# A two-layer cross-attention kernel: the last chunk's layer 0 placed directly behind chunk 6's, ahead of chunk 4's layer 1, with chunk 6's layer 1 behind the last norm and a fourth x2 buffer

## What is computed

```python
# layer 0
qkv = ln(x, g1, be1) @ w_qkv + b_qkv
ckv = context @ w_ckv + b_ckv
k, v = concat(k_self, k_ctx), concat(v_self, v_ctx)
attn = softmax(where(causal or context, q k^T / sqrt(8), -inf)) @ v
x = x + attn
hdn = gelu(ln(ln(x, g2, be2), gf, bf) @ w1 + b1)
x = x + hdn @ w2 + b2
# layer 1
q = ln(x, ln_w, ln_b) @ wq.T + bq;  k, v = context @ wk.T + bk, context @ wv.T + bv
out = softmax(where(mask == 0, -1e9, q k^T / sqrt(8))) @ v @ wo.T + bo + x
```

## Time and profile before

| what | value |
|---|---|
| median of 3 executions | 466.83 us (463.14 to 469.13) |
| the profiled execution, its own time | 466.68 us |
| its span, first to last instruction | 464.7 us |
| around the span | 2.0 us |
| busy share: TensorE matmul / VectorE / ScalarE / GpSimd | 83% / 63% / 56% / 31% |
| mean granted TensorE clock, of full speed | 0.920 |
| instructions | 20173 |

### The profile page before, as it was taken

One profiled execution on the slowest core, in us unless ns is written; L12 is line 12 of the kernel. 1 busy time (PEld: TensorE's weight loads), 2 busy tenths in 40 slices (PEclk: granted clock), 3 DMA queues, 4 the chain that ended last, 5 costly groups with the idle time before them and its releaser, 6 DMA issues.

```text
span 464.7 us, 20173 instructions
## 1 busy us (share of the span) xinstructions
PE 385.1 (83%) x8885; PEld 280.0 (60%) x8885; DVE 293.5 (63%) x733; ACT 261.3 (56%) x451; POOL 142.3 (31%) x209
## 2 busy tenths in 40 slices
PE   3759969996989898979999798969898989587674
PEld 1337747664576666757676667657676677355463
DVE  5435786469569775797469665876389549506331
ACT  2467735653757477555746475646656756435241
POOL 7100634046205520462116320551047106502000
PEclk9975997999999899998999899999899999888856
DMA  6758076017602650185105830284001400310200
GB/s 190 200 152 165 8 183 161 1 70 173 172 4 106 146 165 3 72 171 150 49 13 147 191 91 2 95 172 128 2 26 39 129 1 27 106 34 26 71 25 23
DMA packets 41958, 42.86 MB, mean 92 GB/s; under 512 B 3192, under 2 KB 34376, under 8 KB 41872
## 3 DMA queue, kind: packets, MB, share of 16 engines
q1 hardware_dynamic: 40420, 39.86, 33.3%
q0 software_dynamic: 624, 1.26, 1.0%
q10 hardware_dynamic: 828, 0.46, 0.3%
HBM read 23.65 MB, written 17.83 MB: 89 GB/s over the span
## 4 chain that ended last, share of the span: by engine, by line
PE 53%; DVE 17%; ACT 11%; issue 9%; POOL 5%; DMA 2%; ACTq 1%; SPq 0%; DVEq 0%; POOLq 0%
PE dense L667 12%; PE dense L690 7%; DVE top L971 6%; PE dense L680 4%; PE mixed L850 4%; PE key L820 3%; PE dense L672 3%; PE key L811 3%; PE mixed L858 3%; ACT probs L504 3%; PE side L883 3%; PE query L778 2%; PE query L770 2%; ACT hidden L588 2%; PE dense L662 2%
## 5 line engine op out<-in xcount | busy, mean ns | idle before, releaser
L971 DVE TENSOR_REDUCE top<-query 128x8 f32<-128x1024 f32 (+1 forms) x96 | 117.3, 1222 | 77.0 <-PE query L778 57.2
L504 ACT ACTIVATE probs<-key 128x1024 f32<-128x1024 f32 x96 | 98.3, 1024 | 85.3 <-PE key L820 58.6
L444 POOL TENSOR_TENSOR top<-top 128x8 bf16<-128x8 f32 (+1 forms) x96 | 20.3, 213 | 224.6 <-DVE top L971 223.8
L820 PE MATMUL key<-top_row,spread 48*64 48x128 bf16 x1536 | 48.8, 227 | 2.8 <-ACT top_row L509 1.8
L850 PE MATMUL mixed<-probs,v 128*32 128x128 f32 x1024 | 42.1, 283 | 0.0
L437 POOL TENSOR_TENSOR rstd_x<-var_eps_x,half 128x4 f32<-128x4 f32 x24 | 24.5, 1020 | 55.9 <-DVE var_eps_x L948 55.9
L811 PE MATMUL key<-q_stack,k_stack 48*64 48x128 f16 x1024 | 41.0, 223 | 0.0
L525 ACT COPY o_t<-mixed 128x256 f32<-128x256 f32 x96 | 35.3, 368 | 9.5 <-PE mixed L871 5.1
L667 PE MATMUL dense<-normed_ft,w 128*128 128x512 f32 x64 | 33.5, 647 | 6.4 <-ACT normed_ft L545 5.1
L820 PEld LDWEIGHTS key<-top_row,spread 48*64 48x64 bf16 x1536 | 33.8, 110 | 5.8 <-ACT probs L504 4.1
L509 ACT COPY top_row<-mixed 128x128 bf16<-128x128 bf16 x96 | 27.0, 281 | 15.9 <-PE mixed L871 15.9
(11 more groups left out here) (116 smaller groups left out, 774.0 us busy)
## 6 DMA issues: line engine op xcount, KB each, us to landing
k_stack<-scratch_k SPq DMA_DIRECT2D x16, 384.0 KB, 6.5
q_stack<-scratch_q SPq DMA_DIRECT2D x64, 96.0 KB
scratch_k<-k_part SPq DMA_DIRECT2D x8, 512.0 KB, 2.8
scratch_k<-k_part SPq DMA_DIRECT2D x16, 256.0 KB, 2.6
scratch_q<-q_part SPq DMA_DIRECT2D x16, 256.0 KB, 2.6
k_stack<-scratch_k SPq DMA_DIRECT2D x16, 192.0 KB
x_in<-in_x SPq DMA_DIRECT2D x8, 256.0 KB, 3.5
scratch_q<-q_part SPq DMA_DIRECT2D x16, 128.0 KB, 2.4
```

What stands on the lines that cost most here:

```text
L504: nc.scalar.activation(probs[u.number % 2][:].rearrange("p h q -> p (h q)"), key[:].rearrange("p h x -> p (h x)"), ACT.Exp, scale=SCALE).t ...
L820: ins = nc.tensor.matmul(key[T * n:T * n + T, h, a * P:(a + 1) * P], spread[u.layer][rows, A2 * h + a, T * n:T * n + T], top_row[u.number ...
L971: nc.vector.tensor_reduce(maxima, query[:].rearrange("p h x -> p (h x)").rearrange("p (a k) -> p a k", a=w), AX_X, ALU.max, negate=True).t ...
```

## The change

The fixed offset of twelve steps a chunk gives way to lists with one start for each chunk. Chunks 0 to 5 keep their steps. For the rest:

| | before | after |
|---|---|---|
| U0.7 (layer 0 of the last chunk) | 84 to 91 | 80 to 87 |
| U1.4 | 80 to 83 | 88 to 91 |
| U1.5 | 92 to 95 | 94 to 97 |
| U1.6 | 104 to 107 | 104 to 107 |
| U1.7 | 116 to 119 | 110 to 113 |
| k1.6, k1.7 | 79, 91 | 87, 92 |
| v1.6, v1.7 | 83, 95 | 91, 97 |
| f_t.7 ... w2b.7 | 97 ... 100 | 93 ... 96 |
| norm x2.6, x2_t.6, q1.6 | 91, 92, 93 | 90, 91, 92 |
| norm x2.7, x2_t.7, q1.7 | 103, 104, 105 | 98, 99, 100 |
| last step | 127 | 121 |

x2 has four buffers in place of three, mix_t two in place of one; ScalarE's `mix` waits for the output projection of two chunks before in place of one. Nothing is computed otherwise, and no instruction is added or taken away.

```diff
-SLOTS = 12
-L0_AT = (0, 1, 2, 3, 4, 5, 6, 7)
-L1_AT = (32, 33, 34, 35)
-BACK_AT = (35, 39)
-FIRST, END = -24, SLOTS * (CHUNKS - 1) + 44
+L0 = [12 * c for c in range(CHUNKS - 1)] + [80]
+L1 = [32, 44, 56, 68, 88, 94, 104, 110]
+IN = [12 * c for c in range(CHUNKS)]
+K1 = L0[:6] + [80, 85]
+X2 = L0[:6] + [71, 79]
+V0A, V0B = [s - 16 for s in IN], [s - 14 for s in IN]
+V1 = [s + 11 for s in L0[:6]] + [91, 97]
+BACK_AT = (3, 7)
+FIRST, END = -24, L1[-1] + 12
...
-def due(rel, s):
-
-    c, left = divmod(s - rel, SLOTS)
-    return [c] if left == 0 and 0 <= c < CHUNKS else []
+def due(rel, s, start=L0):
+
+    return [c for c in range(CHUNKS) if start[c] + rel == s]
...
-JOBS = (("f_t", 13), ("w1_0", 13), ("w1_1", 13), ("w1_2", 14), ("w1_3", 14), ("ctx_t", -22), ("w2a", 15),
-        ("k_ctx", -21), ("w2b", 16), ("x_t", -20), ("k0", -19), ("out", 41), ("q0", -18), ("k1", 7), ("x2_t", 20),
-        ("v0a", -16), ("q1", 21), ("v0b", -14), ("v1", 11))
+JOBS = (("f_t", L0, 13), ("w1_0", L0, 13), ("w1_1", L0, 13), ("w1_2", L0, 14), ("w1_3", L0, 14), ("ctx_t", IN, -22),
+        ("w2a", L0, 15), ("k_ctx", IN, -21), ("w2b", L0, 16), ("x_t", IN, -20), ("k0", IN, -19), ("out", L1, 9),
+        ("q0", IN, -18), ("k1", K1, 7), ("x2_t", X2, 20), ("v0a", V0A, 0), ("q1", X2, 21), ("v0b", V0B, 0),
+        ("v1", V1, 0))
...
-        x2 = many(3, "x2", [P, TILES, D])
+        x2 = many(4, "x2", [P, TILES, D])
...
-        mix_t = sb("mix_t", [P, TOK])
+        mix_t = many(2, "mix_t", [P, TOK])
...
-                for c in due(11, s):
+                for c in due(11, s, K1):
                     if c > 0:
                         sp.wait_ge(s_fill["k1"], 48 * c)
...
-                for c in due(22, s):
+                for c in due(22, s, X2):
...
-                for c in due(6, s):
+                for c in due(6, s, K1):
                     pool.wait_ge(s_mask, 16 * (c + 1))
...
                 for c in due(8, s):
                     root(c, "x1")
+                for c in due(8, s, K1):
                     pool.wait_ge(s_high["k1"], c + 1)
...
-                for c in due(19, s):
+                for c in due(19, s, X2):
                     pool.wait_ge(s_norm["x2"], c + 1)
...
-                if c > 0:
-                    act.wait_ge(s_done["out"], c)
+                if c > 1:
+                    act.wait_ge(s_done["out"], c - 1)
```

More of the change, by code:

```diff
@@ L38 @@
 K_HIGH, K_LOW = slice(0, 3, 2), slice(1, 2)
[L48 to L52 removed]
+L0 = [12 * c for c in range(CHUNKS - 1)] + [80]
[7 more added lines that the diff above has]
+FIRST, END = -24, L1[-1] + 12
 ALL = range(FIRST, END)
 Unit = namedtuple("Unit", "layer chunk place number")
[L58 to L61 removed]
+def due(rel, s, start=L0):
+    return [c for c in range(CHUNKS) if start[c] + rel == s]
 UNIT = {}
 for _s in ALL:
[L66 to L68 removed]
+    for _layer, _start, _n in ((0, L0, CB), (1, L1, CB // 2)):
+        for _place in range(_n):
+            for _c in due(_place, _s, _start):
+                assert _s not in UNIT
                 UNIT[_s] = Unit(_layer, _c, _place, len(UNIT) + 1)
@@ L104 @@
     for _rel in BACK_AT:
-        for _c in due(_rel, _s):
+        for _c in due(_rel, _s, L1):
             SIDES.append(("back", _s))
@@ L368, in _ @@
             for s in ALL:
-                for c in due(-18, s):
+                for c in due(-18, s, IN):
                     if c > 0:
@@ L376, in _ @@
                     store_low("k", c, K_LOW, flat[:, 1:2], s_read["k0"])
-                for c in due(-17, s):
+                for c in due(-17, s, IN):
                     if c > 0:
@@ L389, in _ @@
                     fill_queries("q", c, q_stack[c % 2], 0)
-                for c in due(-25, s):
+                for c in due(-25, s, IN):
                     if c >= 2:
@@ L422, in _ @@
                     fill_queries("q1", c, q1_stack[c % 2], 1)
-                for c in due(3, s):
+                for c in due(3, s, K1):
                     if c > 0:
@@ L467, in _ @@
                     split_top(UNIT[s + 3])
-                for c in due(-23, s):
+                for c in due(-23, s, IN):
                     if c > 0:
@@ L487, in _ @@
                         s_k1_low, 1)
-                for c in due(19, s):
+                for c in due(19, s, X2):
                     pool.wait_ge(s_norm["x2"], c + 1)
-                    nc.gpsimd.tensor_tensor(x2[c % 3][:], x2[c % 3][:], rows(row_bo), ALU.add).then_inc(s_x2_bo, 1)
+                    nc.gpsimd.tensor_tensor(x2[c % 4][:], x2[c % 4][:], rows(row_bo), ALU.add).then_inc(s_x2_bo, 1)
                 for c in due(9, s):
@@ L589, in dense @@
                                              bias=cols[:, B1 + f:B1 + f + 1]).then_inc(s_read[f"w1_{f}"], 1)
-                for c in due(8, s):
+                for c in due(8, s, K1):
                     act.wait_ge(s_read["k1"], c + 1)
@@ L627, in _ @@
                 for n, rel in enumerate(BACK_AT):
-                    for c in due(rel, s):
+                    for c in due(rel, s, L1):
                         mix(c, n, s)
@@ L734, in dense @@
                 for c in job_due("out", s):
-                    pe.wait_ge(s_side_read, side_number("back", SLOTS * c + BACK_AT[1]))
-                    by_tokens("out", c, mix_t, w_t[:, 3, :])
+                    pe.wait_ge(s_side_read, side_number("back", L1[c] + BACK_AT[1]))
+                    by_tokens("out", c, mix_t[c % 2], w_t[:, 3, :])
                 for c in job_due("q0", s):
@@ L1033, in statistics @@
                     dve.wait_ge(s_read["w2b"], c + 1)
-                    stats("x2", x2[c % 3], range(TILES))
+                    stats("x2", x2[c % 4], range(TILES))
             def projected(s):
@@ L1076, in projected @@
                         dve.wait_ge(s_out, 16 * c)
-                    nc.vector.tensor_tensor(flat(result), job("out", c)[:], flat(x2[c % 3]), ALU.add).then_inc(
+                    nc.vector.tensor_tensor(flat(result), job("out", c)[:], flat(x2[c % 4]), ALU.add).then_inc(
                         s_read["out"], 1)
```

21 lines of the change are left out of this document (11 added, 10 removed).

## The result

The changed kernel took 476.91 us (median of 4 runs, 475.81 to 477.52), the kernel before 467.2 in the runs beside it (463.14 to 469.13): ratio 1.0192, 95% interval 1.0145 to 1.0238. It is slower by 9.7 us. The prediction was 467.6 with 457 to 475, most of its chance on no change: it was wrong, and the time lies in the rival called half clock, slower than before. In a second series, on another chip, the same kernel took 475.51 (ratio 1.0149, 1.0078 to 1.0220). Some executions lie over 1.5% above the fastest of their kernel; the ratios leave these out, the medians and ranges beside them don't.

What follows compares the result with a forecast made beforehand. TensorE, busy 83% of the span, was taken to set the pace, with the last chunk's chain alone from 395 us. Stage estimates gave 461.5 (full clock) to 473.7 (half clock); the middle, 467.6, was forecast, range 457 to 475.

Steps and rivals of the forecast that it cites:

- half clock, slower than before: Rival: clock falls in step 95 (w2a, w2b take 3.8 more) and again in steps 101 to 103; 473.7 to 477.5, chance 0.21.
- The lead: Last chunk's x1 statistics end at 382.2 against 395.25, 13.0 us ahead; 2.3 left at f_t.7. Rival that keeps it: 453.7, 0.17.
- the walk: Step-by-step estimate through the engines' in-order queues, steps 80 to the end, with new start times.
- the crowd: Steps 88 to 93: chunk 6's x2 and chunk 7's x1 meet on GpSimd and VectorE; f_t.7 20.4 us behind the statistics.
- falling somewhere in steps 101 to 107: Clock assumed to fall among the last units, so the middle between full and half clock, 467.6, was taken; chance 0.42.
- The sum between the marks: Predicted time from the end of chunk 6's x1 statistics (step 79) to the end of the span: 112.8 us.
- the 19.0 of the sum: From f_t.7 to w2b.7's end, with U1.5 inside the MLP: 19.0 us against 12.84 before.
- They cost nothing, since f_t.7 waits for VectorE.: TensorE's waits of 4 and 5 us in steps 91 and 93 bring clock falls, claimed to cost nothing.
- The wait for exp: Inside the MLP, behind the last Gelu with its table load: 2.3 us, by 1.28 and 1.02.
- x2 and q1: From w2b.7's end to x2_t.7 4.3 us against 9.15 before; then q1.7's low part 4.8 after it, as before.
- The tail: Units behind q1.7 end last; U1.7's first query at 439.0 to 445.1, then 23.8 us at half clock to result.7's end.
- full-clock end: Rival, full clock to the end: U1.7's first query at 439.0, result.7 ends at 456.8; 461.5 in all, chance 0.20.

Runs made afterwards that it cites:

- both: Changed kernel with x1.7's second root ahead of the mask, chunk 6's x2 norm, x2_t, q1 three steps later, x2.6's root behind b2: 472.93 us, ratio 1.0082.
- after: The changed kernel itself, unedited, as profiled: 476.91 us, ratio 1.0192 to the kernel before.
- warm_after: Changed kernel with matmuls whose result is never read (the fills) put into TensorE's waits in steps 87 to 112: 467.26 us.
- mlp_alone: Changed kernel with U1.5 four steps later (98 to 101) and v1.7 at step 103: 466.55 us, ratio 0.9956.

## Why the prediction was wrong

**Right: the mechanism up to f_t.7.** The lead came, and the in-order queues of GpSimd and VectorE ate it, with the mask in the chain just ahead of f_t.7, as the walk had it: 20.94 us behind the statistics against 20.4. Taking the crowd apart (both) brought 11.66. k1.6's fill was hidden, and steps 91 and 93 had waits of 6.07 and 2.76 where about 4 and 5 were forecast. The norm of x2.6 took 4.02 and not 1.2, but beside GpSimd's three operations (3.8), which the walk had in the way anyway, so it cost only 0.4: that the stage came out so near is in part luck.

**The lead, -11.1 and not -13.0.** 1.6 of it is the clock: the wait in step 87, 2.05 here, was followed by w2a.6 at half clock, in the timeline of after:

```profile
375.87 3.61 PE L696 MATMUL dense<-w,hidden 128*128 128x128 f32 x16
```

In the five executions in which it ran at full clock the stage took 29.7 against 29.4 predicted, though the wait was the same. The argument that the 1.45 at 375 hadn't brought a fall before was no safety for a longer wait with other work around it.

**The step that failed: the clock, taken as "falling somewhere in steps 101 to 107" and at nothing ahead of them.** The sum between the marks was 112.8, and 121.57 were measured, 8.8 more. Set beside warm_after's stages and rows, 5.5 of these are falls ahead of step 101: 1.6 in step 87, 2.8 in step 95, where the keys and values behind the wait and w2a (3.62 for 1.95) ran at half clock, and 1.1 in q1.7. The rival had named the fall in step 95, at 3.8 for w2a and w2b; I gave it 0.21 and kept it out of the sum. Only w2a was hit: w2b took 1.95. Fills bring the MLP from 21.63 to 17.89, under the 19.0 of the sum (17.6 with w1's first products at full clock), so but for the clock that term was sound.

**"They cost nothing, since f_t.7 waits for VectorE."** For the wait of step 91 this held: the clock fell there and was back at 1.00 ahead of f_t.7, and the chain has no piece of TensorE between x1.7's root and f_t.7. Behind the wait of step 93 it fell too, under w1's first products, which took 3.37 for 1.98. That sentence was wrong by 1.4 us, but the sum wasn't: the 12.84 of the kernel before, from which it started, had the same products at 3.71.

**The wait for exp.** 2.3 were put down for it; it was 3.51, since ScalarE also has the read of k1.7 (k_part, 0.53 in the chain at 413.92) ahead of the table load, and two copies (o_t and top_row, 0.6 with the handing over) between exp and the keys. The table load itself is 1.28, and Exp follows it directly:

```profile
413.92 0.53 ACT k_part L600
414.48 1.28 ACT L510
415.77 1.02 ACT probs L510
```

That is the row's price, as the sum had it. The draining that the Trainium skill (ScalarE: Activation LUTs, "What ACT_TABLE_LOAD costs") adds to it is not seen here either.

**x2 and q1.** 5.04 for 4.3 and 6.11 for 4.8. In x2 the walk had left out a result, now chunk 4's, which still stands between the norm and x2_t.7 in VectorE's order (0.61). Of the 1.3 of q1, 1.1 is the clock again (q1.7 2.05; with fills the stage takes 5.00).

**The tail.** The first query of U1.7 was to come at 439.0 to 445.1 and came at 450.35, 12.1 behind q1.7's low part, inside the 8.3 to 14.4 of the bounds. It waited for units and not for a DMA, as forecast. But the full-clock end was too low: with the clock at 1.00 almost throughout (warm_after) the tail takes 31.08, and 26.1 was the bound: 10.8 in place of 8.3 up to that query, and 20.3 in place of 17.8 behind it. I let the units of steps 101 to 106 go by a query and its maxima, 1.22. The last ones go by ScalarE: exp, the copies of o_t and top_row, then the keys of the next unit, 2.3 us each, as in the timeline of after:

```profile
446.14 0.42 PE L826 MATMUL key<-top_row,spread 48*64 48x128 bf16 x16 [1.03 <-ACT top_row L515]
...
448.44 0.59 PE L826 MATMUL key<-top_row,spread 48*64 48x128 bf16 x16 [1.01 <-ACT top_row L515]
```

**What I chose wrongly.** 19.0 for the MLP stage against 12.84 was in the sum, as the price of U1.5 inside it. It was the second largest loss of the sum, behind the 10.8 up to f_t.7, and was plain before the run; I set it against the lead and didn't ask what it would be worth elsewhere. mlp_alone shows it: 10.9 less in the MLP and the stage ahead of it, for 2.0 more behind. That the sum, 112.8, is so near the 112.46 that the change gives with fills is luck: half of the tail's clock span (12.2) was in the 112.8, and its own full-clock case was 106.7 between the marks, 5.8 under the measured one, 5.0 of it in the tail. The range should have reached to the case that named the clock.

## What to carry to other kernels

A wait of TensorE that hides behind another engine need not be free: the products behind it can start at half clock, so look for the large products behind every new wait (here 2.05 to 6.07 us), price them at double, and ask whether the kernel before paid the same there. When a stage is put ahead, write down the order of every in-order queue at the place where the two chunks now meet, the DMA issuer's too: here q1.6, ready at 407.18, was stored 13 us later behind one that wasn't ready. And keep units that change ScalarE's table out of the last chunk's chain, where nothing covers the load; their place is in the waits that are there anyway.

## What the runs showed of the hardware that was not expected

VectorE's tensor_scalar beside GpSimd's tensor_tensor does not run slower by a part, each piece that meets one waits out that operation: 4.02 for 1.11, above. In both, even the one of four columns a row took 1.04, beside GpSimd's operations, where it is 0.17 elsewhere:

```profile
389.06 1.04 DVE L954 TENSOR_SCALAR var_eps_x<-mean_var_x 128x4 f32<-128x4 f32 x1
```

The clock can stay low under a busy engine: 0.50 in 460 to 464 of after, with TensorE busy 3.86 of 4 us, on small units of 48 rows by 64 columns. Before, it was 4.89 of 6. And the same stretch of the same orders falls or doesn't: w2a.6 took 3.26 to 3.61 us in five executions and 2.05 in five others, behind the same wait of 2.05.

Programs that are the same up to there but for a few steps reached one point between 348.5 and 355.7 us, a scatter of 2%, as large as the effect studied. In the two executions of the changed kernel the stages behind it repeat to some 0.2 us except the tail (1.4).
